# A graph convolution block on one core: linear layers, self rows and batch norm sums moved, tile by tile, into the edge aggregation

## The chip, the cores and the metric

The kernel runs on one core of one Trainium2 chip. The metric is the device time of one execution in microseconds (us). Below, "engine" means TensorE (PE, with its weight loads PEld), VectorE (DVE), ScalarE (ACT), GpSimd (POOL) or the queue of SyncE (SP).

## The reference

There are 6250 nodes with 256 features and 100,000 edges, sorted by destination, each with a weight. The block is a two-layer graph convolution with batch norm, and then a mixture of eight experts:

```python
def gcn_conv(x, src, dst, w, W, b, n):          # src, dst, w include one self edge of weight 1 per node
    xw = x @ W
    deg = segment_sum(w, dst)
    dinv = where(deg > 0, rsqrt(deg), 0.0)
    return segment_sum(xw[src] * (dinv[src] * w * dinv[dst])[:, None], dst) + b

h = layernorm(x)
out = gcn_conv(relu(gcn_conv(h, W1, b1)), W2, b2)
out = (out - out.mean(0)) * rsqrt(out.var(0) + 1e-5) * gamma + beta
x = x + relu(out + h)
x = x + top2_experts(layernorm(x))              # gate, 8 experts, exact gelu
```

## The kernel before, in words

**Tiles.** The nodes are padded to 49 tiles of 128 rows. X holds all tiles with a node per partition (49 x 256 columns), ACC holds the aggregate transposed (a feature per partition, two halves, 49 x 128 columns each). Because aggregation and linear layer commute, each layer first sums rows scaled by `dinv` and then multiplies by the weights.

**Edges.** The edges are cut into 784 tiles of 128, in 56 groups of 14 tiles (GT). A group's destinations span fewer than 128 nodes from a base `base_f[g]` that the data give. The first 16 groups (DG, "dense") go another way than the last 40 (GG, "gathered"):

- *Dense*: their weights are added up per pair (source, destination) and scattered by POOL, 224 indirect DMAs (L479), into a zeroed table in DRAM, which SP had filled (L358). SP reads it back in 196 units of 128x512 (L374, seven slots), and PE multiplies each unit with one tile of X (`dense`, L1272) into banks 6 and 7: 49 units make a block, 4 blocks a layer, and DVE adds a finished block to ACC (`add_block`, L923).
- *Gathered*: POOL fetches the source rows with 14 indirect DMAs per group (L492) into one of two buffers. DVE builds 14 one-hot matrices with the weights (`build`, L908), PE sums the group in 28 matmuls (L1287) into banks 0 to 3, and DVE adds the result to ACC at the group's base (`add_group`, L932). POOL may fill a buffer again once PE has signalled that the group in it is summed (`summed`).

**Order in a group.** The order is written out by hand. For group k DVE runs `build(k+1)`, then any finished block, then waits for `summed` and runs `add_group(k)`. PE runs tile j of the group, and after some of them a dense unit. Before the first group of layer 0 PE does 74 units by themselves (`BEFORE`); after that `PER_GROUP = (4, 5)` units go with each group, so layer 0 has dense units until group 30, and layer 1 until group 39.

**Around a layer.** Layer 0 begins with rows of X scaled by DVE and ACT, their store to a table in DRAM by SP (L381), and the self rows: PE transposes each tile of X (L1260, banks 4 and 5) and DVE copies it to ACC (L901). After its last group comes the linear layer, one tile after another: PE multiplies (L1308, banks 6 and 7), DVE scales and adds the bias into `tmp` (L971), ACT applies relu and scales into X (L623). Every seven tiles SP stores a chunk of X (L386). POOL's gathers of layer 1 wait for the last of these stores. The self rows of layer 1 follow on PE and DVE in the same way as before.

After the last group of layer 1 come the linear layer (L1308, DVE L982 back into ACC), with POOL adding up the rows (L512); PE reduces the sum (L1322), DVE forms the mean (L988) and subtracts it from ACC (L992), ACT squares (L632), PE adds up the squares (L1322), DVE forms the variance (L995), ACT takes the root (L635), DVE the reciprocal (L997) and the scale (L998, L1006). For the residual ACT rebuilds the normalized input (L644), POOL adds beta (L519), DVE adds the two (L1011). Router and experts follow, unchanged by the diff.

**The start.** Duplicate pairs within the dense edges are found by comparing each key with its 40 neighbours (MAXIN), eight at a time, in five passes on DVE: compare (L781), weights of equal ones (L783), a maximum over the eight (L784) and a sum over the eight (L787); L789 to L791 combine the passes. From this come the cells and weights that POOL scatters (L794 to L807). DVE and PE then sum the degrees group by group (L839 to L847, L1224), while POOL scatters.

Of the kernel before, what the change touches and what calls it, by code (L numbers as in the profile page):

```python
# [23 lines left out]
ASLOTS = 7  # L24
LN_EPS = 1e-05
# [25 lines left out]
def gnn_ffn(nc, x, src, dst, edge_weight, g_W1, g_b1, g_W2, g_b2, g_gamma, g_beta,  # L51
# [27 lines left out]
    UNITS = NB * NT  # L79
    GG = NG - DG  # L80
# [8 lines left out]
    with ExitStack() as ctx:  # L89
# [20 lines left out]
        parts = arena[:, at + 8 * RW:at + (8 + MAXIN // 8) * RW]  # L110
        assert (8 + MAXIN // 8) * RW <= 2 * GT * P
# [32 lines left out]
        eq8 = early(8 * (HALO + RW))  # L144
        had = early(MAXIN // 8 * RW)
# [59 lines left out]
        b1rows, sd_b = ln, mean_b  # L205
# [43 lines left out]
        sum_done, centred, sq_ready, sq_used = sem("sum_done"), sem("centred"), sem("sq_ready"), sem("sq_used")  # L249
# [18 lines left out]
        Q = NT  # L268
        BEFORE = (74, 0)
        PER_GROUP = (4, 5)  # L270

        def units_of(layer):
            

            n, plan = BEFORE[layer], []
            for g in range(GG):
                m = min(PER_GROUP[layer], UNITS - n) if g < GG - 1 else UNITS - n
                plan.append((n, m))
                n += m
            return plan  # L280
        SLOT_CH = [(NCH + 1) // 2, NCH // 2]
# [23 lines left out]

        def prior(q, j):


            return q + 1 if j == 0 else q
# [7 lines left out]
        with nc.Block() as block:  # L317
# [3 lines left out]
            def _(sp):  # L321
# [62 lines left out]
                for c in range(NCH):  # L384
                    sp.wait_ge(y_ready, 1 + CH * (c + 1))
# [51 lines left out]
            def _(pool):  # L437
# [66 lines left out]
                pool.wait_ge(agg_done, 2)  # L504
                g.memset(tmp[:, :], 0.0).then_inc(z_added, 1)
                with pool.Fori(0, NCH) as c:
                    for j in range(CH):
                        q = c * CH + j
                        pool.wait_ge(lin_used, q + (Q + 2))
                        pool.wait_ge(z_added, prior(q, j))  # L510
                        z = tmp[:, (j % 2) * D:(j % 2 + 1) * D].rearrange("p (c n) -> p c n", c=KC)
                        g.tensor_tensor(z, z, acc[:, :, bass.ds(q * P, P)], ALU.add).then_inc(z_added, 1)  # L512


# [57 lines left out]
            def _(act):  # L572
# [42 lines left out]
                act.sem_inc(y_ready, 1)  # L615
                for c in range(NCH):
                    for j in range(CH):
                        t = CH * c + j
                        if c + j == 0:
                            for n in range(2):  # L620
                                act.wait_ge(y_stored[n], 16 * SLOT_CH[n])
                        act.wait_ge(lin_used, 1 + t + 1)
                        a.activation(X[:, t * D:(t + 1) * D], tmp[:, (j % 2) * D:(j % 2 + 1) * D], ACT.Relu,  # L623
                                     scale=dinv[:, t:t + 1]).then_inc(y_ready, 1)


                with act.Fori(0, NCH) as c:
                    act.wait_ge(centred, c * 2 + 2)
                    for j in range(CH):
                        q = c * CH + j  # L630
                        act.wait_ge(sq_used, q + 1)
                        a.activation(slot(j).rearrange("p (c n) -> p c n", c=KC),  # L632
                                     acc[:, :, bass.ds(q * P, P)], ACT.Square).then_inc(sq_ready, 1)
                act.wait_ge(bn_var, 1)
                a.activation(sd_b[:, :], sd_b[:, :], ACT.Sqrt).then_inc(bn_sd, 1)  # L635
# [17 lines left out]

                norm_x(0)
                norm_x(1)
# [55 lines left out]
            def _(dve):  # L711
# [14 lines left out]
                dve.sem_inc(lin_used, 1)  # L726
# [24 lines left out]
                seen, first = eq8[0:DR, 0:RH], eq8[0:DR, RH:2 * RH]  # L751
# [429 lines left out]
            def _(pe):  # L1181
# [131 lines left out]
                for c in range(NCH):  # L1313
                    for j in range(CH):
                        linear(0, CH * c + j, j, W1g)
# [134 lines left out]
```

## Time and profile before

| | us |
|---|---|
| three executions, median (lowest, highest) | 3095.94 (3092.03, 3101.72) |
| the profiled execution | 3096.93 |
| its span, first to last instruction | 3095.1 |
| busy in it: PE, PEld | 2158.0, 1539.0 |
| busy in it: POOL, DVE, ACT | 1676.4, 901.8, 377.0 |
| mean granted clock of TensorE, share of full speed | 0.889 |

No engine is busy throughout, so the shares alone say little: the profile has to be read stage by stage. The rows quoted below are from the view of busy time by stretch and from timelines of single engines. In a timeline a row gives the start, the duration, the engine, the line, the operation with output and input, how often it is merged in the row, and in square brackets the idle time of the engine before it and what ended it. "Remote" means that the releaser is not among the recorded work, and "issue" that the engine waited for nothing that the profile shows. Starts are us from the beginning of the span.

### The profile page before, as it was taken

To read this page: it belongs to the slowest core of one execution; us is meant where nothing else is said; L and a number is where in the kernel's file an instruction comes from. 1 tells how busy PE (TensorE), PEld (TensorE's weight loads), DVE (VectorE), ACT (ScalarE), POOL (GpSimd) and SP (SyncE) were. 2 spreads that over 40 slices of the span, in tenths; PEclk is the share of its full clock that TensorE was granted. 3 is DMA by queue.
4 is the path that set the end of the run, shared out by engine and by line. 5 is a ranking of instruction groups with operands and counts; after the bars stand their busy time and mean duration, and the time that the engine had idled before them with its cause. 6 is when DMAs were issued, how large, how long until landed. Compare 5 with 4: busy or idle time off the path is not lost.

```text
span 3095.1 us, 34624 instructions
## 1 busy us (share of the span) xinstructions
PE 2158.0 (70%) x10692; PEld 1539.0 (50%) x10693; DVE 901.8 (29%) x2587; ACT 377.0 (12%) x1053; POOL 1676.4 (54%) x1782
## 2 busy tenths in 40 slices
PE   0100046998888788646598788888888666899897
PEld 0100033455555555535365455555555562788887
DVE  8700055011222211212332212222123676233332
ACT  6000001000000000001200000000000562333333
POOL 1677703016666666663346666666665430566665
PEclk9999999998888888767889899999999755999999
DMA  9940005544544444332445555555555023677775
GB/s 325 329 144 1 0 0 163 158 136 143 145 145 141 143 142 144 95 92 80 131 123 158 147 154 157 156 155 155 153 160 168 24 77 103 169 189 175 180 176 135
DMA packets 264392, 431.24 MB, mean 139 GB/s; under 512 B 39664, under 2 KB 147887, under 8 KB 264143
## 3 DMA queue, kind: packets, MB, share of 16 engines
q1 hardware_dynamic: 181455, 253.80, 26.1%
q0 software_dynamic: 81088, 173.80, 21.9%
q10 hardware_dynamic: 1728, 2.13, 0.2%
q8 instruction: 64, 1.05, 0.1%
q14 instruction: 57, 0.47, 0.0%
HBM read 339.36 MB, written 91.16 MB: 139 GB/s over the span
## 4 chain that ended last, share of the span: by engine, by line
another core or an unknown queue 28%; PE 23%; POOL 17%; DVE 13%; issue 11%; DMA 6%; POOLq 1%; DVEq 1%; SPq 1%; ACT 1%; ACTq 0%
POOL arena L492 14%; PE psum L1272 8%; PE psum L1287 4%; DMA ACC<-rows_for_experts,ACC 4%; DVE arena L908 3%; PE psum L1308 3%; PE psum L1394 2%; PE psum L1402 2%; POOL out_dram L558 2%; PE psum L1369 2%; DMA out_dram<-ACC 1%; PE psum L1224 1%; DVE ACC L845 1%; PE psum L1322 1%
## 5 line engine op out<-in xcount | busy, mean ns | idle before, releaser
L492 POOL DMA_INDIRECT arena<-conv_rows,edge_cols x1120 | 1059.4, 946 | 887.7 <-issue 318.7
L1287 PEld LDWEIGHTS psum<-arena 128*128 128x128 f32 x4480 | 640.9, 209 | 501.6 <-issue 484.8
L1287 PE MATMUL psum<-arena 128*128 128x128 f32 x4480 | 683.4, 296 | 289.9 <-issue 277.3
L1272 PE MATMUL psum<-arena,X 128*128 128x512 f32 x1568 | 815.5, 653 | 43.6 <-DVE ACC L923 26.4
L1272 PEld LDWEIGHTS psum<-arena,X 128*128 128x128 f32 x1568 | 303.3, 211 | 307.3 <-issue 273.3
L932 DVE TENSOR_TENSOR ACC<-ACC,psum 128x256 f32 x80 | 33.8, 422 | 1226.0 <-remote 1085.4
L479 POOL DMA_INDIRECT pair_weights<-scale_b,mean_b x224 | 229.5, 1025 | 156.3 <-DVE mean_b L807 88.3
L908 DVE TENSOR_SCALAR arena<-iota,edge_cols 128x128 f32<-128x128 f32 x1120 | 294.4, 370 | 0.3
L1224 PE MATMUL psum<-ACC 128*128 128x6 bf16 x784 | 56.1, 202 | 318.1 <-DVE ACC L845 299.0
L1394 PE MATMUL psum<-ACC,arena 128*128 128x128 f32 x1680 | 215.8, 284 | 0.2 <-DVE ACC L1154 0.2
L1224 PEld LDWEIGHTS psum<-ACC 128*128 128x128 bf16 x784 | 51.5, 159 | 322.8 <-DVE ACC L845 303.2
L558 POOL DMA_INDIRECT out_dram<-ACC x105 | 167.7, 1597 | 74.2 <-issue 49.2
L1394 PEld LDWEIGHTS psum<-ACC,arena 128*128 128x128 f32 x1680 | 206.8, 201 | 0.6 <-issue 0.6
L1402 PE MATMUL psum<-arena,ACC 128*128 x840 | 199.9, 381 | 0.2 <-ACT ACC L689 0.2
L1402 PEld LDWEIGHTS psum<-arena,ACC 128*128 128x128 f32 x840 | 152.7, 192 | 17.2 <-issue 0.6
L546 POOL DMA_INDIRECT ACC<-rows_for_experts,ACC x105 | 104.9, 999 | 84.8 <-DVE ACC L1141 51.0
L623 ACT ACTIVATE X<-tmp,dinv 128x256 f32<-128x256 f32 x49 | 24.9, 508 | 991.1 <-DVE tmp L971 991.1
L689 ACT ACTIVATE ACC<-psum,b1e 128x128 f32<-128x128 f32 x420 | 119.8, 369 | 164.5 <-PE psum L1394 130.8
L632 ACT ACTIVATE edge_cols<-ACC 128x256 f32 x49 | 18.8, 413 | 915.4 <-DVE ACC L992 914.8
L1172 DVE TENSOR_TENSOR ACC<-psum,b2e 128x256 f32<-128x256 f32 x105 | 44.7, 426 | 267.9 <-PE psum L1402 211.8
L842 DVE COPY ACC<-psum 128x6 f32 x56 | 9.1, 162 | 275.0 <-remote 263.2
L1260 PE MATMUL psum<-ident,X 128*128 128x128 f32 x196 | 50.3, 384 | 52.0 <-DVE ACC L901 27.3
(259 smaller groups left out, 1410.3 us busy)
## 6 DMA issues: line engine op xcount, KB each, us to landing
arena<-pair_weights SPq DMA_DIRECT2D x392, 256.0 KB
arena<-in_L_ffn_W_dram SPq DMA_DIRECT2D x113, 512.0 KB, 7.8
pair_weights<-zeros SPq DMA_DIRECT2D x4, 12544.0 KB, 60.5
arena<-conv_rows,edge_cols POOLq DMA_INDIRECT x1120
conv_rows<-X SPq DMA_DIRECT2D x14, 896.0 KB, 4.8
X<-in_x_dram SPq DMA_DIRECT2D x12, 896.0 KB, 10.4
rows_for_experts<-ACC SPq DMA_DIRECT2D x7, 910.0 KB, 4.3
out_dram<-X SPq DMA_DIRECT2D x6, 896.0 KB
```

What stands on the lines that cost most here:

```text
L479: pool.indirect_dma_start(pairs, bass.IndirectOffsetOnAxis(cell_i[:, t:t + 1], 0), cell_w[:, t:t + 1], None).then_inc(paired[b], 16)
L492: pool.indirect_dma_start(G[:, n * D:(n + 1) * D], None, y_tab[layer], bass.IndirectOffsetOnAxis(srcT[:, t:t + 1], 0)).then_inc(gathered[n ...
L546: pool.indirect_dma_start(xs[:, u * DX:(u + 1) * DX], None, rows_x, bass.IndirectOffsetOnAxis(slot_i[:, n:n + 1], 0)).then_inc(xs_in[u], 16)
L558: pool.indirect_dma_start(out, bass.IndirectOffsetOnAxis(slot_i[:, n:n + 1], 0), ys[:, u * D:(u + 1) * D], None, bounds_check=N - 1, oob_i ...
L689: ins = a.activation(hT[:, slot * H + c * P:slot * H + (c + 1) * P], psum[:, 2 + slot, c * P:(c + 1) * P], ACT.Gelu, bias=b1e[:, bass.ds(e ...
L908: v.tensor_scalar(S[:, n * P:(n + 1) * P], iota[:, 0:P], dst_rel[:, t:t + 1], wT[:, t:t + 1], ALU.is_equal, ALU.mult).then_inc(s_ready, 1)
L1224: ins = m.matmul(bank(2 + h, 6), hot[:, :, j], w_group[:, (h * GT + j) * 6:(h * GT + j + 1) * 6], start=(j == 0), stop=(j == GT - 1))
L1272: ins = m.matmul(bank(6 + c, BW), X[:, t * D + c * P:t * D + (c + 1) * P], A_in[:, u * BW:(u + 1) * BW], start=(t == 0), stop=(t == NT - 1))
L1287: ins = m.matmul(bank(2 * (k % 2) + c, P), G[:, n * D + c * P:n * D + (c + 1) * P], S[:, n * P:(n + 1) * P], start=(j == 0), stop=(j == GT ...
L1308: ins = m.matmul(bank(6 + j % 2, D), acc[:, k, bass.ds(q * P, P)], W[:, k * D:(k + 1) * D], start=(k == 0), stop=(k == KC - 1))
L1394: ins = m.matmul(psum[:, 2 + s, c * P:(c + 1) * P], w1s[:, s4 * KC * H + k * H + c * P:s4 * KC * H + k * H + (c + 1) * P], xsT[:, s * D + ...
L1402: ins = m.matmul(bank(4 + s, D), hT[:, s * H + c * P:s * H + (c + 1) * P], w2e[:, bass.ds(e * (HC * D) + c * D, D)], start=(c == 0), stop= ...
```

## The change

1. **Linear layers inside the aggregation.** Groups of edges are sorted by destination, so a tile of ACC is complete once the groups and dense blocks that reach it are added. `finish_of` works out, from a pace of 112 nodes a group (PACE) with a slack of 80, in which group each tile can be finished. In layer 0 that is from group 25 on (all four blocks must be in), three tiles a group, 45 in all; 4 remain for after the last group. In layer 1 it is from group 4 on, mostly one tile a group, three in groups 10, 20 and 30, 40 in all; 9 remain. PE does a tile's `linear` after edge tile j = 2, 6 or 10 of the group, in banks 4 and 5. DVE runs `finish` after `build(k+1)` and before `add_group(k)`. A new check sets the flag for the general path if a group's base is over 80 nodes off the pace.
2. **Next self rows.** With tile i of layer 0's linear layer PE also transposes the finished tile i-3 of X (banks 6 and 7), and DVE copies it to ACC. Only the last three are left for after.
3. **Dense units.** `PER_GROUP` becomes (5, 5), so that layer 0's dense work ends at group 24.
4. **Batch norm sums with a shift.** The mean of layer 1's first finished tile is subtracted from that tile, and from the bias of all later ones. DVE adds up the rows and the squares (which ACT makes) tile by tile. At the end two pairs of matmuls reduce both, and the variance is E[z^2] - E[z]^2. The subtraction of the mean, the pass of squares and POOL's sums are gone; the mean goes into beta instead, so that POOL's addition of beta now waits for the scale.
5. **Tree sums for duplicates.** The compare result becomes bf16, and the reductions over eight become three additions (maxima) of halves and one into a running result.

```diff
+SLACK = 80
+    PACE = GT * P * N // E
-        PER_GROUP = (4, 5)
+        PER_GROUP = (5, 5)
+        TURN_LAG = 3
 # duplicates (DVE), in each of the five passes
                     chain(v.tensor_tensor(same, key[:, 0:SPAN].unsqueeze(1).broadcast_to([DR, 8, SPAN]),
                                           sliding(key, d0, 8, 1, SPAN), ALU.is_equal))
                     v.tensor_tensor(wsame, same[:, :, HALO:SPAN], sliding(wrow, HALO + d0, 8, 1, RW), ALU.mult)
-                    chain(v.tensor_reduce(had[0:DR, c * RW:(c + 1) * RW],
-                                          sliding(eq8[0:DR, :], HALO - d0, 8, SPAN - 1, RW).rearrange("p d i -> p i d"),
-                                          AX_X, ALU.max))
-                    chain(v.tensor_reduce(parts[0:DR, c * RW:(c + 1) * RW], wsame.rearrange("p d i -> p i d"),
-                                          AX_X, ALU.add))
-                v.tensor_reduce(eq8[0:DR, 0:RW], had[0:DR, :].rearrange("p (c i) -> p i c", i=RW), AX_X, ALU.max)
-                chain(v.tensor_reduce(eqw[0:DR, 0:RW], parts[0:DR, :].rearrange("p (c i) -> p i c", i=RW), AX_X, ALU.add))
-                v.tensor_tensor(eqw[0:DR, RW:2 * RW], eqw[0:DR, 0:RW], wrow[:, HALO:SPAN], ALU.add).then_inc(pairs_summed, 1)
+                    chain(v.tensor_tensor(had3[:, 0:4], sliding(eq8[0:DR, :], HALO - d0, 4, SPAN - 1, RW),
+                                          sliding(eq8[0:DR, :], HALO - d0 + 4 * (SPAN - 1), 4, SPAN - 1, RW), ALU.max))
+                    v.tensor_tensor(had3[:, 4:6], had3[:, 0:2], had3[:, 2:4], ALU.max)
+                    chain(v.tensor_tensor(wsame[:, 0:4], wsame[:, 0:4], wsame[:, 4:8], ALU.add))
+                    v.tensor_tensor(had3[:, 6], had3[:, 4], had3[:, 5], ALU.max)
+                    chain(v.tensor_tensor(wsame[:, 0:2], wsame[:, 0:2], wsame[:, 2:4], ALU.add))
+                    v.tensor_tensor(had[0:DR, :], had3[:, 6], had3[:, 6] if c == 0 else had[0:DR, :], ALU.max)
+                    chain(v.tensor_tensor(wsame[:, 0], wsame[:, 0], wsame[:, 1], ALU.add))
+                    chain(v.tensor_tensor(wsum[0:DR, :], wsame[:, 0], wrow[:, HALO:SPAN] if c == 0 else wsum[0:DR, :],
+                                          ALU.add))
+                v.tensor_copy(had_f[0:DR, :], had[0:DR, :]).then_inc(pairs_summed, 1)
 # DVE, tile by tile
+                def finish(layer, i):
...
+                    dve.wait_ge(lin_done, n + 1)
+                    if layer == 0:
+                        if i >= 2:
+                            dve.wait_ge(y_ready, i - 1)
+                        v.scalar_tensor_tensor(out=tmp[:, (i % 2) * D:(i % 2 + 1) * D], in0=bank(4 + n % 2, D),
+                                               scalar=dinv[:, t:t + 1], in1=b1g[:, :],
+                                               op0=ALU.mult, op1=ALU.add).then_inc(lin_used, 1)
+                        if i >= TURN_LAG:
+                            take_self(1, i - TURN_LAG, FINISH[0][0][i - TURN_LAG], 6)
+                    else:
...
+                            dve.wait_ge(lin_used, n + 1)
+                            dve.wait_ge(z_added, i)
+                            z = z_sum.rearrange("p (c n) -> p c n", c=KC)
+                            v.tensor_tensor(z, z, out_rows, ALU.add).then_inc(z_added, 1)
+                            add_square(i - 1)
...
+                            for i in FINISH[layer][1][k]:
+                                finish(layer, i)
                             add_group(k)
                         dve.wait_ge(added, GG * (layer + 1))
+                        v.memset(dscr[:, :], 0.0).then_inc(agg_done, 1)
+                        finish_rest(layer, NT - len(FINISH[layer][2]), chain_fast)
 # PE, tile by tile
+                def linear(layer, i):
+                    t, n, W = FINISH[layer][0][i], NT * layer + i, (W1g, W2g)[layer]
+                    if n >= 2:
+                        pe.wait_ge(lin_used, n - 1)
...
+                    if layer == 0 and i >= TURN_LAG:
+                        turn_self(1, i - TURN_LAG, FINISH[0][0][i - TURN_LAG], 6)
...
+                                if j % 4 == 2 and j // 4 < len(FINISH[layer][1][k]):
+                                    i = FINISH[layer][1][k][j // 4]
+                                    blocks = NB if layer == 0 else blocks_under(FINISH[1][0][i])
+                                    if DG * layer + blocks:
+                                        pe.wait_ge(dense_added, DG * layer + BG * blocks)
+                                    linear(layer, i)
 # scale (DVE); POOL's additions of beta wait for bn_set
                 dve.wait_ge(sum_done, 2)
+                chain(v.tensor_scalar(mean_b[:, :], bank(6, D), 1.0 / N, None, ALU.mult))
+                chain(v.tensor_tensor(scale_b[:, :], mean_b[:, :], mean_b[:, :], ALU.mult))
+                chain(v.scalar_tensor_tensor(out=scale_b[:, :], in0=bank(7, D), scalar=1.0 / N, in1=scale_b[:, :],
+                                             op0=ALU.mult, op1=ALU.subtract))
+                chain(v.tensor_scalar(scale_b[:, :], scale_b[:, :], 0.0, BN_EPS, ALU.max, ALU.add))
+                v.tensor_copy(dscr[:, :], zeros[:, 0:1]).then_inc(bn_var, 1)
                 dve.wait_ge(bn_sd, 1)
-                chain(v.reciprocal(scale_b[:, :], sd_b[:, :]))
+                chain(v.reciprocal(scale_b[:, :], sd_b))
                 chain(v.tensor_tensor(scale_b[:, :], scale_b[:, :], gam[:, :], ALU.mult))
+                chain(v.tensor_tensor(mean_b[:, :], mean_b[:, :], scale_b[:, :], ALU.mult))
+                v.tensor_tensor(bet[:, :], bet[:, :], mean_b[:, :], ALU.subtract).then_inc(bn_set, 1)
```

## Rows read from the trace of the kernel before

**Rows 1.** Busy time by stretch: from, to, length; PE, PEld, DVE, ACT, POOL (count), clock, DMA.
```profile
674.00:1450.00 776.00, 579.98 (x2659) 410.77 (x2657) 158.06 (x584) 0.00 (x0) 503.25 (x532) 0.81 0.44 128
1571.00:2352.00 781.00, 652.36 (x2949) 428.57 (x2948) 157.50 (x582) 0.00 (x0) 502.44 (x532) 0.92 0.52 152
```
**Rows 2.** Timeline of DVE, two groups of layer 0 and two of layer 1.
```profile
875.73 0.42 DVE L932 TENSOR_TENSOR ACC<-ACC,psum 128x256 f32 x1 [16.18 <-remote]
895.96 0.42 DVE L932 TENSOR_TENSOR ACC<-ACC,psum 128x256 f32 x1 [16.22 <-remote]
...
1610.83 0.42 DVE L932 TENSOR_TENSOR ACC<-ACC,psum 128x256 f32 x1 [16.20 <-remote]
...
1631.07 0.42 DVE L932 TENSOR_TENSOR ACC<-ACC,psum 128x256 f32 x1 [16.23 <-remote]
```
**Rows 3.** Timeline of POOL at the end of one group's gathers in layer 1.
```profile
1627.21 0.95 POOL L492 DMA_INDIRECT arena<-conv_rows,edge_cols  x1 [0.30 <-issue]
1631.21 0.95 POOL L492 DMA_INDIRECT arena<-conv_rows,edge_cols  x1 [3.05 <-remote]
```
**Rows 4.** Timeline of DVE, the last groups of layer 0, eight group intervals apart.
```profile
1299.62 0.42 DVE L932 TENSOR_TENSOR ACC<-ACC,psum 128x256 f32 x1 [12.57 <-remote]
...
1449.76 0.42 DVE L932 TENSOR_TENSOR ACC<-ACC,psum 128x256 f32 x1 [9.39 <-PE psum L1287]
```
**Rows 5.** Timelines of DVE, ACT and POOL between the layers.
```profile
1452.18 0.48 DVE L971 SCALAR_TENSOR_TENSOR tmp<-psum,dinv,b1g 128x256 f32<-128x256 f32 x1 [1.33 <-PE psum L1308]
...
1501.48 0.51 ACT L623 ACTIVATE X<-tmp,dinv 128x256 f32<-128x256 f32 x1 [0.43 <-DVE tmp L971]
...
1507.76 0.94 POOL L492 DMA_INDIRECT arena<-conv_rows,edge_cols  x1 [65.67 <-DMA conv_rows<-X]
...
1570.52 0.94 POOL L492 DMA_INDIRECT arena<-conv_rows,edge_cols  x1 [28.03 <-PE psum L1287]
```
**Rows 6.** Timeline of DVE, self rows of layer 1 before and during POOL's gathers.
```profile
1504.41 0.76 DVE L901 COPY ACC<-psum 128x256 f32<-128x256 f32 x2 [0.26 <-PE psum L1260]
...
1542.94 0.42 DVE L901 COPY ACC<-psum 128x256 f32<-128x256 f32 x1 [4.48 <-remote]
```
**Rows 7.** Timelines of DVE and POOL after the last group of layer 1.
```profile
2357.69 0.06 DVE L961 MEMSET dscr<- 128x1 f32 x1 [0.60 <-DVE ACC L932]
2359.80 0.48 DVE L982 SCALAR_TENSOR_TENSOR ACC<-psum,dinv,b2g 128x256 f32 x1 [2.05 <-PE psum L1308]
...
2440.05 1.75 DVE L997 RECIPROCAL scale_b<-mean_b 128x256 f32<-128x256 f32 x1 [0.48 <-ACT mean_b L635]
2440.58 10.44 POOL L519 TENSOR_TENSOR edge_cols<-edge_cols,bet 128x256 f32<-128x256 f32 x10 [28.43 <-ACT edge_cols L644]
2447.39 3.06 DVE L1011 TENSOR_TENSOR edge_cols<-edge_cols,ACC 128x896 f32<-128x896 f32 x2 [2.05 <-POOL edge_cols L519]
```
**Rows 8.** Timeline of DVE at the start: one pass for duplicates, the end, a bf16 product.
```profile
28.16 2.68 DVE L781 TENSOR_TENSOR ACC<-arena 112x2432 f32<-112x2432 f32 x1
...
33.09 3.62 DVE L784 TENSOR_REDUCE ACC<-ACC 112x256 f32<-112x2048 f32 x1
36.74 3.65 DVE L787 TENSOR_REDUCE arena<-arena 112x256 f32<-112x2048 f32 x1
40.42 2.69 DVE L781 TENSOR_TENSOR ACC<-arena 112x2432 f32<-112x2432 f32 x1
...
89.36 2.31 DVE L789 TENSOR_REDUCE ACC<-ACC 112x256 f32<-112x1280 f32 x1
...
94.27 0.39 DVE L796 SCALAR_TENSOR_TENSOR arena<-psum,edge_cols 128x224 f32<-128x224 f32 x1
...
260.16 1.09 DVE L845 TENSOR_TENSOR ACC<-ACC 128x1792 bf16<-128x1792 bf16 x1
```
**Rows 9.** Timeline of POOL: a scatter beside L829 and one beside no DVE work.
```profile
105.22 2.82 POOL L479 DMA_INDIRECT pair_weights<-scale_b,mean_b  x1 [0.30 <-issue]
...
182.24 0.96 POOL L479 DMA_INDIRECT pair_weights<-scale_b,mean_b  x1 [0.30 <-issue]
```

More of the change, by code:

```diff
@@ L280, in units_of, with finished, blocks_under, finish_of @@
             return plan
+        def finished(g):
+            return NT if g == NG else max(0, min(NT, (PACE * g - SLACK) // P))
+        def blocks_under(t):
+            g = next(g for g in range(NG + 1) if finished(g) > t)
+            under = [d for d in range(min(g, DG)) if PACE * d + SLACK + P > P * t]
+            return under[-1] // BG + 1 if under else 0
+        def finish_of(layer):
+            plan = units_of(layer)
+            ends = [next((k for k, (n, m) in enumerate(plan) if n + m >= (b + 1) * NT), GG - 1) for b in range(NB)]
+            ends = [-1 if (b + 1) * NT <= BEFORE[layer] else e for b, e in enumerate(ends)]
+            free = []
+            for t in range(NT):
+                g = next(g for g in range(NG + 1) if finished(g) > t)
+                blocks = NB if layer == 0 else blocks_under(t)
+                free.append(max(g - DG + 1, ends[blocks - 1] + 1 if blocks else 0, 0))
+            order = sorted(range(NT), key=lambda t: (0 if layer == 0 else min(free[t], GG), t))
+            groups, n = [], 0
+            for k in range(GG):
+                most = 1 if layer == 1 and n == 0 else 2 if k in ends else 3
+                if layer == 1 and n == 1 and groups[-1]:
+                    most = 0
+                mine = []
+                while n < NT and len(mine) < most and free[order[n]] <= k:
+                    mine.append(n)
+                    n += 1
+                groups.append(mine)
+            return order, groups, list(range(n, NT))
+        FINISH = [finish_of(layer) for layer in range(2)]
         SLOT_CH = [(NCH + 1) // 2, NCH // 2]
@@ L501, in _ @@
                                 bass.IndirectOffsetOnAxis(gstg[:, 0:1], 0)).then_inc(gen_gathered, 16)
[L504 to L512, printed above, removed]
+                pool.wait_ge(bn_set, 1)
                 for c in range(NCH):
@@ L1207, in _ @@
                 pe.wait_ge(pairs_summed, 1)
-                for x, rows in enumerate((eq8[0:DR, 0:RW], eqw[0:DR, RW:2 * RW])):
+                for x, rows in enumerate((had_f[0:DR, :], wsum[0:DR, :])):
                     for h in range(2):
@@ new lines, in mean_of_first, with linear_rest @@
+                def mean_of_first():
+                    t = FINISH[1][0][0]
+                    pe.wait_ge(lin_used, NT + 1)
+                    m.matmul(bank(4 + (NT + 1) % 2, D).rearrange("p (c n) -> p c n", c=KC), ones[:, :],
+                             acc[:, :, t * P:(t + 1) * P], start=True, stop=True).then_inc(first_mean, 1)
+                def linear_rest(layer, first):
+                    for i in range(first, NT):
+                        if layer == 1 and i == 1:
+                            mean_of_first()
+                        linear(layer, i)
+                    if layer == 0:
+                        for i in range(NT - TURN_LAG, NT):
+                            turn_self(1, i, FINISH[0][0][i], 6)
```

227 lines of the change are left out of this document (126 added, 101 removed).

## Prediction

> **What bounds the kernel now.** The view of busy time by stretch comes first. In both aggregations [rows 1] no engine is full: over 781 us of layer 1 PE is busy 652, POOL 502, DVE 158, ACT 0. So what counts is what a group waits for, and the rest of the time lies in stretches where one engine works alone. DVE's timeline shows how long a group is: two `add_group` of layer 0, with four dense units between them, stand 20.23 us apart, two of layer 1, with five, 20.24 [rows 2]. A fifth unit costs nothing, so PE's work isn't the limit. POOL's timeline shows what is [rows 3]: a gather occupies 0.95 us and 0.30 us of issue, 14 of them 17.5 us, and before the first gather of the next group POOL stands 3.05 us, 2.75 more than between two others; 17.5 + 2.75 = 20.25. It waits for the signal that PE has summed the group before. That DVE's wait ends by "remote" says that PE's signal came later than its recorded work. Where dense units are gone, at the end of layer 0, eight intervals take 150.14 us, 18.8 each [rows 4].
>
> Between the layers POOL stands still. From layer 0's last addition (1449.76) to the first gather of layer 1 (1507.76) are 58.0 us: 49 tiles of linear layer at 1.0 us each, then 6.3 us from the last relu over the store to the gather [rows 4, 5]. The third set of gathers starts 62.8 us after the first [rows 5]: PE first turned 49 self rows, with a handshake of 0.5 us a tile before the gathers run and 4.5 us during them [rows 6], and only then summed group 0. After layer 1's last group 82.4 us pass until the reciprocal [rows 7]. At the start 12.26 us go to each of five passes over duplicates, and 4.9 us to the end of them [rows 8]; POOL's scatter waits for that, and the rest of the program for the scatter or for DVE's degree loop, which starts behind the same work.
>
> **The change, part by part.** The sum is made against the profiled execution, 3096.93 us; the median of the three is 1.0 lower.
>
> *Duplicates.* Each pass loses two reductions, 3.62 + 3.65 = 7.27 us. It gains two operations of 1024 columns, two of 512 and four of 256. At the rate between L796 (224 columns, 0.39) and L781 (2432, 2.68), 0.16 us + 1.04 ns a column, that is 2 x 1.22 + 2 x 0.69 + 4 x 0.42 = 5.5 us: 1.8 saved, 9 in five passes. If the four bf16 maxima run at L845's rate (1792 columns in 1.09), they cost 1.5 us instead of 2.75, and 6 more are saved. The end goes from 4.9 to a copy of 0.3. The new check on group bases adds five operations of one to 56 columns, about 1.1 us. Together -12 to -19; I take **-15**, as nothing else waits there. Scatter and degree loop both move with it.
>
> *Layer 0's groups.* Five units instead of four cost nothing by [rows 2]. Groups 25 to 39 lose their dense units, but each gets three linear layers, three transposes and the handshakes PE to DVE to ACT. They are no longer than a group with five units (20.2), if the 18 us of a group hold three handshakes; no shorter than 18.8. Before, nine groups ran at 18.8. At 20.2 for all, the eight intervals cost 8 x 1.4 = **+11**; at 18.8 for all, six further groups gain 6 x 1.4 = 8. I take +11, since PE's late signals, not its load, made the 20.2. The other bound is a later gather: the handshake of 4.5 us [rows 6] three times is 13.5, which still fits in 20.2 beside DVE's 14 one-hots (3.7 us), but not with much to spare; +34 if each of the 15 groups grows by half of one such handshake.
>
> *Between the layers.* 58.0 becomes four tiles at 1.2 us with their self rows, 1.4 to the first and one to the last relu, and 6.3 for store and gather: 13.8, so **-44**. SP's earlier stores go out during the groups; its loads of dense units for layer 1 stand behind the last store in its queue as before. Bounds -48 (last chunk's store alone) and -35 (the 6.3 doubled by seven tiles to store).
>
> *First groups of layer 1.* Only three self rows come after. Group 0 is summed while group 1 is gathered, so the third set starts two periods after the first: 2 x 20.2 = 40 instead of 62.8, **-23** (-25 to -10: in the first period PE also begins dense units).
>
> *Layer 1's groups.* 40 tiles of linear layer go in: a few matmuls each on PE, which a fifth unit shows to be no limit. DVE: `finish` 0.48, z 0.42, square 0.42, beside 16 us of idle a group; its wait for `linear` lies between `build(k+1)` and `add_group(k)`, so what queues behind it is `add_group`, whose bank PE does not want for the next group. ACT had nothing. What may cost is POOL. A scatter that ran beside DVE's L829 (two inputs in SBUF) took 2.82 us, one beside none 0.96 [rows 9], a stretch of up to 0.67 of L829's 2.77. Adding rows (z, squares) are such operations, 80 in all of 0.42 us; `add_group`, with one input in PSUM, is not. 80 x 0.15 = **+12**; 0 if POOL's 3.05 us of waiting takes it up, +22 at 0.67 x 0.42 each, +50 if each holds POOL for a gather's half.
>
> The Trainium skill speaks against this part ("SBUF — State Buffer", "Who interferes with whom"): a VectorE instruction with two inputs in SBUF contends with a GpSimd instruction that reads SBUF, and a holder of the shared ports blocks the other for its whole length. By it each of the 80 would hold POOL for up to 0.42 us, 34 us, and the sum would be 22 higher; [rows 9] agree with a stretch, and at 1.9 of 2.8 us not with the whole length.
>
> *After layer 1.* 82.4 us become 2.1 to the first result [rows 7], nine tiles at 0.48 + 0.42 + 0.42 + some 0.13 between = 13.0, last square 0.9, two pairs of matmuls 1.7, four small operations on the mean and variance 1.9, root 0.5: 20.3, so **-62**. Against it, POOL's addition of beta ran while DVE made the scale; the first seven tiles (1.04 us each) now begin only when the shifted beta is there. L1011 came 7.3 us after the reciprocal's start; now 1.75 + 0.4 + 0.9 + 7.3 = 10.4 or a little more, **+4**. Bounds for both: -64 to -48 (nine tiles at 2.6 if ACT's squares are waited for singly).
>
> Sum: -15 + 11 - 44 - 23 + 12 - 58 = **-117**: 3096.9 - 117 = 2980 for the profiled execution, 2979 for the median.
>
> **The rivals.** (1) *The groups grow.* Late signals of PE and shared ports make each of layer 1's 40 groups, or layer 0's last 15, longer by 0.5 to 1.5 us: +30 to +65 over the forecast, 3010 to 3045. For it: the pause of 3.05 shows that the signal is on the path, and each `linear` adds waits in PE's queue ahead of it. Against: the fifth unit cost nothing. (2) *The groups without dense units keep their pace* of 18.8, and adds cost nothing: 11 + 8 + 12 less, about 2948. For it: [rows 4]; against: late signals. (3) *Slower.* The three handshakes in each of layer 0's groups 25 to 39 are in series on PE: `linear(i)` waits for DVE to empty the bank two tiles back, DVE for PE's late signal and for ACT. If such a signal arrives only when POOL's issue pauses, a group needs an extra turn of gathers, 20.2 us; 15 x 20.2 = 303 on the sum gives 3283. It decides from 117 / 15 = 7.8 us a group. For it: 4.5 us a handshake, and PE's signals that come only in POOL's pauses; against: [rows 6] already ran under gathers, so the delay is a few us, not a whole period. (4) *The change doesn't take hold*: a base over 80 off the pace sends all to the general path; bases of 112 a group by evenly spread destinations make that remote, and it would be many times slower.
>
> **How the numbers follow.** Forecast 0.68 (its own range 2955 to 3008, from the bounds of the terms, few of which will lie at the same end), rival 1 0.18, rival 2 0.07, rival 3 with smaller kin 0.06, rival 4 0.01. A difference of 0.3%, 9 us, is what a measurement of this kernel can tell. All but rivals 3 and 4 are beyond it on the fast side: faster 0.93, same 0.01, slower 0.06. The range 2945 to 3035 takes in rival 2 and most of rival 1, and leaves out the rest.
>
> **What would show it.** L796 at some 79 us instead of 94.27. `add_group` 20.2 apart throughout, also in groups 25 to 39. From layer 0's last addition to the next gather 14 us, third set of gathers 40 us later. L492 near 0.95 us on average in layer 1; well over 1.0 would mean the ports. From the memset after layer 1 to the reciprocal 20 us. Group intervals above 21 us, or waits of DVE for `lin_done` that end after the last gather of a group, would say that rival 1 or 3 holds; a gap of 30 us or more between the layers would make my view of the stores wrong.

## The result, and the profile after

The changed kernel took 2994.11 us (median of four, 2982.97 to 2998.0) against 3098.29 for the kernel before on the same chip: a ratio of 0.9663, interval 0.9638 to 0.9687. The profiled execution took 2998.0 us (span 2996.2), 99 less than that of before.

The timelines of DVE and POOL at the start of the changed kernel answer to [rows 8]: one pass for duplicates with its tree sums, the first scatter, and the last step of the degree loop.

```profile
26.87 2.68 DVE L818 TENSOR_TENSOR ACC<-arena 112x2432 bf16<-112x2432 f32 x1
...
31.80 0.69 DVE L821 TENSOR_TENSOR ACC<-ACC 112x1024 bf16<-112x1024 bf16 x1
...
32.86 1.22 DVE L824 TENSOR_TENSOR arena<-arena 112x1024 f32<-112x1024 f32 x1
...
36.17 2.69 DVE L818 TENSOR_TENSOR ACC<-arena 112x2432 bf16<-112x2432 f32 x1
...
76.58 1.28 POOL L520 DMA_INDIRECT pair_weights<-scale_b,mean_b  x1 [67.58 <-DVE mean_b L846]
...
399.46 0.16 DVE L881 COPY ACC<-psum 128x6 f32 x1 [9.23 <-remote]
...
455.29 0.16 DVE L881 COPY ACC<-psum 128x6 f32 x1
...
487.18 0.99 POOL L533 DMA_INDIRECT arena<-conv_rows,edge_cols  x1 [115.27 <-DMA conv_rows<-X]
```

A pass is 9.30 us instead of 12.26; maxima in bf16 take little over half of the f32 additions of the same size (0.69 against 1.22). POOL's first scatter starts at 76.6 instead of 97.3. But the first gather, at 487.2, is only 12.2 us earlier than before (499.4).

The view of busy time by stretch, for both aggregations, answers to [rows 1], with the same columns.

```profile
664.00:1447.00 783.00, 611.43 (x2914) 438.42 (x2913) 192.48 (x669) 22.64 (x45) 504.04 (x532) 0.85 0.46 134
1500.00:2327.00 827.00, 699.18 (x3111) 460.77 (x3109) 209.61 (x710) 16.68 (x40) 504.90 (x532) 0.90 0.49 145
```

The timelines of DVE, POOL and ACT answer to [rows 2] to [rows 5]: two groups early in layer 1, two later ones, and what lies between the layers.

```profile
1447.86 0.42 DVE L1032 TENSOR_TENSOR ACC<-ACC,psum 128x256 f32 x1 [0.84 <-PE psum L1406]
...
1453.28 0.51 ACT L651 ACTIVATE X<-tmp,dinv 128x256 f32<-128x256 f32 x1 [0.57 <-DVE tmp L950]
...
1460.21 1.05 POOL L533 DMA_INDIRECT arena<-conv_rows,edge_cols  x1 [24.19 <-DMA conv_rows<-X]
...
1540.53 0.42 DVE L1032 TENSOR_TENSOR ACC<-ACC,psum 128x256 f32 x1 [16.33 <-remote]
...
1560.76 0.42 DVE L1032 TENSOR_TENSOR ACC<-ACC,psum 128x256 f32 x1 [16.21 <-remote]
...
1830.39 0.42 DVE L1032 TENSOR_TENSOR ACC<-ACC,psum 128x256 f32 x1 [13.50 <-PE psum L1406]
...
1854.78 0.42 DVE L1032 TENSOR_TENSOR ACC<-ACC,psum 128x256 f32 x1 [15.66 <-PE psum L1406]
1854.92 0.95 POOL L533 DMA_INDIRECT arena<-conv_rows,edge_cols  x1 [7.21 <-PE psum L1406]
```

The gap between the layers is gone: 12.4 us from the last addition to the first gather instead of 58.0. Early groups of layer 1 stand 20.23 us apart, as before. From about 1830 on they don't: 24.39 here. And the wait is named otherwise: POOL waits 7.21 us, and what ends it is no longer "remote", a late signal, but PE's matmul itself. In the stretch of layer 1 above, 21 of POOL's waits end that way, 107.0 us in all, and 17 by "remote"; in the kernel before it was 3 and 35. From 1830.5 to the last set of gathers at 2294.2 the sets start 20.3 to 28.1 us apart, 22.1 on average.

DVE's timeline after the last group answers to [rows 7].

```profile
2327.90 0.06 DVE L1053 MEMSET dscr<- 128x1 f32 x1
2330.01 0.48 DVE L957 SCALAR_TENSOR_TENSOR ACC<-psum,dinv,mean_b 128x256 f32<-128x256 f32 x1 [2.04 <-PE psum L1355]
...
2340.97 0.95 DVE L975 TENSOR_TENSOR tmp<-tmp,ln 128x256 f32<-128x256 f32 x2
...
2348.74 0.42 DVE L1075 TENSOR_SCALAR mean_b<-psum 128x256 f32<-128x256 f32 x1 [6.82 <-PE psum L1443]
...
2351.08 1.75 DVE L1082 RECIPROCAL scale_b<-ln 128x256 f32<-128x256 f32 x1 [0.48 <-ACT ln L684]
...
2360.82 3.05 DVE L1098 TENSOR_TENSOR edge_cols<-edge_cols,ACC 128x896 f32<-128x896 f32 x2 [4.08 <-POOL edge_cols L550]
```

By stage, from the two traces, against the terms of the forecast:

| stretch | before | after | change | forecast |
|---|---|---|---|---|
| start to the first gather | 499.4 | 487.2 | -12.2 | -15 |
| to layer 0's last addition | 950.3 | 960.7 | +10.4 | +11 |
| to the first gather of layer 1 | 58.0 | 12.4 | -45.6 | -44 |
| to the third set of gathers | 62.8 | 39.9 | -22.9 | -23 |
| to layer 1's last addition | 786.2 | 827.4 | +41.2 | +12 |
| to the reciprocal | 83.4 | 23.7 | -59.7 | -62 |
| to the end | 655.1 | 645.1 | -10.0 | +4 |

One term is far off: layer 1's groups.

### The profile page after: what moved, and what is told of

It reads as the page before. It is cut to its first block, busy times and chain, and to the rows that moved or that the text cites. A ratio compares the mean times of both kernels' runs of the same rounds, so it can differ in the third digit from the quotient of the medians.

```text
span 2996.2 us, 34126 instructions
## 1 busy us (share of the span) xinstructions
PE 2110.1 (70%) x10594; PEld 1505.7 (50%) x10595; DVE 903.2 (30%) x2713; ACT 378.4 (13%) x1053; POOL 1639.9 (55%) x1732
## 4 chain that ended last, share of the span: by engine, by line
PE 43%; another core or an unknown queue 23%; DVE 13%; issue 11%; DMA 6%; POOL 3%; POOLq 1%; DVEq 1%; ACT 1%; SPq 0%; ACTq 0%
PE psum L1391 17%; PE psum L1406 13%; DMA ACC<-rows_for_experts,ACC 4%; PE psum L1355 3%; DVE arena L1008 3%; PE psum L1510 2%; PE psum L1518 2%; POOL out_dram L589 2%; PE psum L1485 2%; PE psum L1344 1%; DMA out_dram<-ACC 1%; DVE ACC L884 1%; PE psum L1310 1%; PE psum L1501 1%
## 5 line engine op out<-in xcount | busy, mean ns | idle before, releaser
L1406 PEld LDWEIGHTS psum<-arena 128*128 128x128 f32 x4480 | 629.0, 207 | 390.1 <-issue 380.1
L1406 PE MATMUL psum<-arena 128*128 128x128 f32 x4480 | 663.5, 293 | 202.8 <-issue 189.5
L1510 PE MATMUL psum<-ACC,arena 128*128 128x128 f32 x1680 | 208.3, 277 | 0.2 <-DVE ACC L1241 0.2
L1510 PEld LDWEIGHTS psum<-ACC,arena 128*128 128x128 f32 x1680 | 198.9, 194 | 0.6 <-issue 0.6
L661 ACT ACTIVATE ln<-ACC 128x256 f32<-128x256 f32 x49 | 20.4, 417 | 866.8 <-issue 520.1
L1355 PE MATMUL psum<-W1g,ACC 128*128 128x256 f32 x196 | 71.4, 474 | 31.8 <-issue 17.3
## 6 DMA issues: line engine op xcount, KB each, us to landing
X<-in_x_dram SPq DMA_DIRECT2D x12, 896.0 KB, 10.4
```

The lines of the kernel that those rows point to most:

```text
L1355: ins = m.matmul(bank(4 + n % 2, D), acc[:, k, t * P:(t + 1) * P], W[:, k * D:(k + 1) * D], start=(k == 0), stop=(k == KC - 1))
L1406: ins = m.matmul(bank(2 * (k % 2) + c, P), G[:, n * D + c * P:n * D + (c + 1) * P], S[:, n * P:(n + 1) * P], start=(j == 0), stop=(j == GT ...
L1510: ins = m.matmul(psum[:, 2 + s, c * P:(c + 1) * P], w1s[:, s4 * KC * H + k * H + c * P:s4 * KC * H + k * H + (c + 1) * P], xsT[:, s * D + ...
```

## The experiments

Theory A: PE is too full in layer 1. Rival B: DVE's new additions, with two inputs in SBUF, hold POOL. Rival C: the groups are longer for another reason that has nothing to do with the linear layers. The runs fell on four chips, none of them that of the first measurement: e1 to e4 on one, b2, e5 and e6 on the second, e7, b3 and e8 on the third, e9 on the last. Ratios are to the kernel before on the same chip. Where e1 to e4 and e9 are compared with the changed kernel, that stands on another chip, b2_after's or b3_after's.

**e1_lin1_last**

```diff
                 groups.append(mine)
+            if layer == 1:
+                return order, [[] for _ in range(GG)], list(range(NT))
```

> The changed kernel with all 49 linear layers of layer 1 after the last group, with the shifted sums as they are; layer 0 as changed. Theory A (PE is too full: a linear layer added to a group with five dense units and the pause of some 3 us near the end of each group's gathers pushes PE past the 20.2 us that the gathers take): the groups of layer 1 go back to 20.2 to 20.3 us, third set of gathers to last addition 786 us instead of 827, the 40 tiles moved behind the last group cost 40 x 1.2 = 48 us there. In all +7 (+2 to +12) against the changed kernel. Rival B (the adds of DVE with two inputs in SBUF slow POOL): the same numbers, so this run alone does not part the two. Rival C (the groups of layer 1 are longer for another reason, e.g. the earlier start against the stream of dense units): groups stay at 827, and the run is +48.

**e2_no_adds**

```diff
-                            v.tensor_tensor(z, z, out_rows, ALU.add).then_inc(z_added, 1)
+                            v.tensor_tensor(z_sum[:, 0:1], z_sum[:, 0:1], out_rows[:, 0, 0:1], ALU.add).then_inc(z_added, 1)
-                        v.tensor_tensor(sq_sum, sq_sum, sq, ALU.add).then_inc(sq_used, 1)
+                        v.tensor_tensor(sq_sum[:, 0:1], sq_sum[:, 0:1], sq[:, 0:1], ALU.add).then_inc(sq_used, 1)
```

> The changed kernel, with DVE's additions of rows and of squares cut to one column each (the sums for the batch norm are left out but for that column). Theory A (PE too full): the groups stay long, 820 to 830 us from the third set of gathers to the last addition, and only some 6 us go after the last group, where DVE's three operations a tile set the pace: -4 to -10 in all. Rival B (DVE's adds hold POOL or DVE): back to 786 to 792, -40 to -50 in all.

**e3_spread16**

```diff
-        BEFORE = (74, 0)
+        BEFORE = (74, 16)
-                m = min(PER_GROUP[layer], UNITS - n) if g < GG - 1 else UNITS - n
+                m = min(PER_GROUP[layer] - (layer == 1 and g % 2 == 1), UNITS - n) if g < GG - 1 else UNITS - n
```

> The changed kernel with 16 dense units of layer 1 ahead of its first group, and then five and four units in turn instead of five. Theory A: PE has idle time between the last self row and the first gathered tile (12 us), which takes some six units; the other ten push group 0 by at most 19 us, of which part is cover; with 4.5 units a group on average PE fits in 20.2, so the groups take 790 to 800 instead of 827 and the whole is -15 to -35. Rival B or C: the groups stay near 827, and the whole is 0 to +15.

**e4_dup_old**: the tree sums back to the two reductions a pass and the two at the end, in f32, as in the diff read backwards.

> The changed kernel with the reductions of before for the duplicates. The first scatter comes 20 us later (97). If the degree loop's own queue of halves left over at the scatter's end is the reason that only 12 of the 21 us were kept, the first gather comes 12 (8 to 21) us later and the run is +12. If the loss of 8 us had another cause, it is +20.

The first thing measured was not asked for: on this chip the kernel before took 2610.78 us, not 3098. Signals were prompt: but for one wait of 8.3 us in e3 POOL never waited for PE, and a group took its 14 gathers, 17.5 us. So A could show only if PE were too full even for that, and what is expected above for late signals could not be tested. All further runs met chips of this kind.

| run | ratio (interval) | third gathers to last addition | last addition to reciprocal |
|---|---|---|---|
| e1_lin1_last | 0.9686 (0.9657 to 0.9716) | 680.9 | 72.7 |
| e2_no_adds | 0.9505 (0.947 to 0.9539) | 681.0 | 23.0 |
| e3_spread16 | 0.954 (0.9509 to 0.957) | 681.1 | 23.2 |
| e4_dup_old | 0.9585 (0.9555 to 0.9615) | 683.2 | 23.6 |

For comparison both kernels were traced on the next chip, together with the same undoing for layer 0 and a milder form of e3.

> The kernel before once more, for a trace on this chip. In the four runs above PE's signals were not late and a group took 17.5 us, the time of its 14 gathers, instead of 20.2; the kernel before took 2611 us beside them, not 3098. Expected on such a chip: groups of 17.5 us in both layers, degree loop over long before the scatter ends, 58 us between the layers, 83 us from the last addition to the reciprocal. On a chip as in the prediction: the rows of the prediction.

> The changed kernel once more. On a chip with groups of 17.5 us: the duplicates are then off the path only if the degree loop were, so their 20 us are kept whole; between the layers -44, first groups of layer 1 -20, layer 1's groups 681 us from the third set of gathers to the last addition with or without linear layers in them (0), end -60: some -125 against the kernel before on this chip, ratio 0.952, and about 20 us under the run with the old duplicates. On a chip as in the prediction: ratio 0.966.

**e5_lin0_last**: as e1_lin1_last, with `layer == 0`.

> The changed kernel with all 49 linear layers of layer 0, and the self rows that go with them, after the last group; layer 1 as changed. The gap between last addition and first gather goes from 12 back to 58 us or more, since the transposes now go beside (45 tiles at 1.0 to 1.2 us: +45 to +54). Groups 25 to 39 of layer 0: on a chip with groups of 17.5 us they stay at 17.4 (0); on a chip as in the prediction they go from 19.2 to 18.8 on average (-6). In all +40 to +54.

**e6_spread6**: as e3_spread16, with `BEFORE = (74, 6)` and `g % 4 == 3`.

> The changed kernel with six dense units of layer 1 ahead of its first group, and then four units in every fourth group, five in the others. On a chip as in the prediction, theory A (PE too full): the six units cost nothing, as PE stands idle for 12 us there, and the groups take 800 to 815 us instead of 827: -12 to -27. On a chip with groups of 17.5 us POOL's gathers are the bound, not PE: 0 (-4 to +4).

| run | time, us | ratio (interval) | last addition to first gather | third gathers to last addition |
|---|---|---|---|---|
| b2_before | 2610.84 | | 59.5 | 678.7 |
| b2_after | 2482.10 | 0.9513 (0.948 to 0.9545) | 12.3 | 682.0 |
| e5_lin0_last | 2532.21 | 0.9717 (0.9687 to 0.9747) | 63.2 | 681.6 |
| e6_spread6 | 2476.81 | 0.9497 (0.9467 to 0.9526) | 12.4 | 679.4 |

What follows. On such chips the change gives 4.9% and not 3.4. Its traces put -18.8 us on the start, -47.2 on the gap between the layers, nothing on the first gathers of layer 1 (35.3 before, 35.1 after, where I had expected -20: the self rows had not held them up), +3.3 on layer 1's groups and -62.9 up to the reciprocal. Taking the linear layers of layer 1 out of the groups costs 48.7 us behind them and gives back 1 (e1); those of layer 0 cost 50.9 (e5); the old reductions start the first gather at 392.3 instead of 372.1 and cost 0.7% (e4). So the start and both linear layers are worth close to what was forecast for them. Whether an unfinished degree loop ate 8 of the 20 us at the start of the first chip, which e4 was to tell, it can't tell here: the gathers follow the scatter at once. Sixteen units ahead of layer 1 are too many: the third set of gathers came 43.1 us after the first instead of 35.1 (e3).

Rival B has fallen on both kinds of chip. The view of costliest groups gives the mean of one gather (line, engine, operation, busy us, mean ns, idle before them and what ended it), here for the changed kernel in the first measurement and then on the second chip.

```profile
L533 POOL DMA_INDIRECT arena<-conv_rows,edge_cols x1120 | 1062.6, 949 | 876.8 <-issue 318.2 <-PE psum L1406 261.0 <-remote 158.2
```

```profile
L533 POOL DMA_INDIRECT arena<-conv_rows,edge_cols x1120 | 1066.1, 952 | 357.4 <-issue 340.9 <-DMA conv_rows<-X 16.5
```

In layer 1 alone, in the first measurement, a gather took 949 ns in the changed kernel and 945 before it: 560 x 4 ns = 2 us, not 12 or more. The additions do hold POOL, but briefly and seldom: the 52 gathers beside one took 976 ns on average and 1197 at most. And on the prompt chip e2, without the additions, left the groups at 681.0, as e1 and e3 did. The Trainium skill ("SBUF — State Buffer", "Who interferes with whom"), by which each addition could have held POOL for its 0.42 us, gave too much here: 80 of them cost some 2 us. The idle time shows the other matter: 261 us of POOL waiting for PE's own work (141 of them before the third set of layer 0, where the kernel before has 139) and 158 for late signals on the first chip, while neither is listed on the second.

For A there remained the question how full PE is. Two kernels load it on purpose.

**e7_double_linear**

```diff
-                    for k in range(KC):
+                    for k in range(KC if layer == 0 else 2 * KC):
+                        k = k % KC
```

> The changed kernel with every linear layer of layer 1 computed twice over into the same bank (1.0 us more on PE for each tile, the result the same). Theory A (PE too full), on a chip with groups of 17.5 us: PE's own work in a group is then 9.4 (five dense units) + 7 (14 tiles) + 2 = 18.4 us at full clock, over the 17.5 of the gathers, so the groups take 700 to 730 us from the third set of gathers to the last addition instead of 682, and nine tiles after it 3 us more: +20 to +50. On a chip as in the prediction: +30 to +60 over the changed kernel. If PE had room in a group, as the prediction took it, +3 on either.

**e9_four_linear**: the same with `4 * KC`.

> The changed kernel with every linear layer of layer 1 computed four times over into the same bank (2.6 us more on PE a tile, the result the same); the double one had left the groups at 17.5 us. By the steps of the timeline a group is 14/3 x 1.34 + 4.9 x 1.72 = 14.7 us of PE, 15.5 with one linear layer, 16.4 with two, 18.1 with four. Theory A's reading (PE limits the groups once its own time with its pauses passes that of the gathers) on a chip with groups of 17.5 us: 0.6 us on each of 40 groups and a backlog at blocks' ends, third set of gathers to last addition 700 to 715 instead of 682, and 2.6 us on nine tiles after it, 23: +40 to +60 in all. On a chip as in the prediction, where the pauses take 3 us of a group and the lower clock some 2: +90 to +120 in the groups. If PE were not what a group can come to wait for: +23 in all.

e7: 0.9556 (0.9532 to 0.958), the groups 683.5 us, hardly longer than without it, and 27.8 from the last addition to the reciprocal. My expectation of +20 to +50 missed. These two stretches are 4.5 us longer than in b3_after, close to the +3 expected if PE has room; the medians differ by 11 us with intervals that overlap. I had given PE too much time for a group. e9: 0.9734 (0.9713 to 0.9754), the groups 719.6, then 40.0, 37.6 and 16 us more than in b2_after. Here POOL waited for PE 20 times, 41.4 us in all: the load has become the bound. In all e9 is 59 us over b2_after, within the expected +40 to +60, though its groups passed the expected 700 to 715. DVE's timeline of e9 in layer 1 shows PE's own pace with four linear layers, and that of the kernel before on the second chip its pace with none, while it still had units to catch up on:

```profile
1514.57 0.42 DVE L1032 TENSOR_TENSOR ACC<-ACC,psum 128x256 f32 x1 [5.37 <-PE psum L1407]
...
1532.86 0.42 DVE L1032 TENSOR_TENSOR ACC<-ACC,psum 128x256 f32 x1 [8.88 <-PE psum L1407]
...
1551.15 0.42 DVE L1032 TENSOR_TENSOR ACC<-ACC,psum 128x256 f32 x1 [8.88 <-PE psum L1407]
```

```profile
1204.88 0.42 DVE L932 TENSOR_TENSOR ACC<-ACC,psum 128x256 f32 x1 [10.73 <-PE psum L1287]
...
1219.72 0.42 DVE L932 TENSOR_TENSOR ACC<-ACC,psum 128x256 f32 x1 [10.81 <-PE psum L1287]
...
1234.56 0.42 DVE L932 TENSOR_TENSOR ACC<-ACC,psum 128x256 f32 x1 [10.73 <-PE psum L1287]
```

18.29 us with four, 14.84 with none, so 0.86 for each linear layer, and 15.7 us for the changed kernel's group on PE at full clock (granted 1.00 in the stretches of these rows).

The busy time of layer 1's stretch on the second chip, the changed kernel and then the kernel before, with the columns of [rows 1]:

```profile
1127.00:1809.00 682.00, 625.89 (x3064) 420.74 (x3062) 207.75 (x696) 16.69 (x40) 506.58 (x532) 0.99 0.60 175
```

```profile
1193.00:1872.00 679.00, 604.79 (x2936) 396.79 (x2934) 158.09 (x578) 0.00 (x0) 505.23 (x532) 0.98 0.60 176
```

Nearly the same work took PE 626 us there and 699 on the first chip, 73 us or 1.8 a group more, at a granted clock of 0.99 against 0.90; for the kernel before it was 48 us (652.4 against 604.8), 1.2 a group. On the first chip PE also stands idle, 128 us in the stretch of layer 1 (827 - 699; in the kernel before 781 - 652 = 129). Much of this lies near the end of each set of gathers, where its matmuls come one by one. This timeline of PE in the kernel before shows it, beside a set whose gathers ran from 1897.55 to 1914.73:

```profile
1910.33 1.05 PE L1287 MATMUL psum<-arena 128*128 128x128 f32 x8
1911.22 1.88 PE L1272 MATMUL psum<-arena,X 128*128 128x512 f32 x4
1912.94 0.38 PE L1287 MATMUL psum<-arena 128*128 128x128 f32 x2
1913.78 0.27 PE L1287 MATMUL psum<-arena 128*128 128x128 f32 x1 [0.46 <-issue]
1914.52 0.35 PE L1287 MATMUL psum<-arena 128*128 128x128 f32 x1 [0.47 <-issue]
1915.88 0.27 PE L1287 MATMUL psum<-arena 128*128 128x128 f32 x1 [1.02 <-issue]
1917.28 1.23 PE L1287 MATMUL psum<-arena 128*128 128x128 f32 x7 [1.13 <-issue]
```

The row of 1910.33 ends the group; the matmuls that come one by one are already the next group's first. In the changed kernel (gathers from 1809.30 to 1826.50) the group's last two tiles fall into this pause, and PE starts again at half the pace (3.62 us for the four matmuls of a unit, which otherwise take 1.88):

```profile
1824.83 0.27 PE L1406 MATMUL psum<-arena 128*128 128x128 f32 x1
1826.24 0.48 PE L1406 MATMUL psum<-arena 128*128 128x128 f32 x2 [1.14 <-issue]
1828.33 0.37 PE L1406 MATMUL psum<-arena 128*128 128x128 f32 x1 [1.61 <-issue]
1829.04 1.22 PE L1406 MATMUL psum<-arena 128*128 128x128 f32 x4 [0.34 <-issue]
1830.05 3.62 PE L1391 MATMUL psum<-arena,X 128*128 128x512 f32 x4
1833.46 1.76 PE L1406 MATMUL psum<-arena 128*128 128x128 f32 x12
1835.05 1.88 PE L1391 MATMUL psum<-arena,X 128*128 128x512 f32 x4
```

These terms must not be added up and held against the 20.2 us: busy and idle time together fill any stretch, and 15.7 + 1.8 + 3.2 is only 827 / 40 again. What tells the room is how long before its signal arrives, that is, before `add_group`, a group's last matmul has ended:

| groups on the first chip | last matmul to `add_group`, us |
|---|---|
| before, layer 0, 8 to 29 (four units) | 8.2 (median) |
| before, layer 1, 3 to 8 (five units) | 6.3 (median) |
| after, layer 0, 15 to 23 (five units) | 6.1 (median) |
| after, layer 1, up to 15, one linear layer, away from a block's end (eight groups) | 4.1 to 5.7 |
| after, layer 1, 16 to 36 | 0.1 to 0.6 in 19 of 21 |

Each load brings the end closer to the signal, the fifth unit (1.72 us) too. In the rows of the kernel before the pause begins at 1913.3, 4.3 us before `add_group` at 1917.61, so by my estimate some 2 of the 6.3 us were room, and with a linear layer at most 1.4 were left. Once these are used up, the last matmuls of a group come to lie in the pause, POOL starts its next 14 gathers later, and what a block's addition adds in waiting (PE stood idle for 8.41 us at 1898, behind DVE) is not made good. That is theory A. Against rival C speak the groups without a linear layer: five units alone kept to 20.2 or 20.3 us in layer 0 but behind the ends of two blocks, and behind late group 36 group 37, which has none, was 5.2 us ahead of its signal again. All this is argued from that chip's trace and from PE's times on the others; no kernel could be run against it on a chip with late signals, so it isn't shown, and rival C isn't excluded there. Why signals are late on one chip and not on others, and what holds PE's matmuls up in the pauses, stays open as well.

Last, the milder spreading once more beside the changed kernel.

> The changed kernel once more, beside the next run. 0.951 of the kernel before on a chip with groups of 17.5 us, 0.966 on one as in the prediction.

> Six dense units of layer 1 ahead of its first group once more, for a closer comparison with the changed kernel on the same chip. On a chip with groups of 17.5 us: 3 to 8 us under the changed kernel, from the third set of gathers to the last addition 679 instead of 682. On a chip as in the prediction, by theory A 12 to 27 under it.

Changed kernel 2486.35 us, 0.9516 (0.9491 to 0.954); with six units ahead 2483.64, 0.9496 (0.9477 to 0.9516), groups of layer 1 680.5 against 682.7. Both times it was the faster one, by 5 and by 3 us, but the intervals overlap: no difference is shown. On a chip with late signals, where it would matter by theory A, it wasn't run.

## Why the prediction was right, and where not

The time, -99 us in the profiled execution against -117, and 2994 in a range of 2945 to 3035, was right; its terms were so in part, and luck had a share: half of the 29 us by which layer 1's groups missed was made up by the last stretch, 14 us under its term.

- *Between the layers* and *first groups of layer 1*: -45.6 and -22.9 for -44 and -23, by the steps given. The second exists only where handshakes during the gathers are slow; on the other chips it is nothing.
- *After layer 1*: -59.7 for -62. Two errors nearly cancel: a tile took 1.2 us instead of 1.45, and the matmuls for the two sums came after a wait of 6.8 us instead of 1.7. POOL's addition of beta cost 2.4 (9.7 from reciprocal to L1098 instead of 7.3) for 4.
- *Duplicates*: -20.7 at the first scatter, beyond the range of -12 to -19. The passes gave 14.7, as the maxima did run at bf16's rate, their end 4.7, and they began 1.3 earlier instead of 1.1 later. "Scatter and degree loop both move with it" failed on the first chip. While POOL scatters, DVE waits up to 37.9 us for a signal of PE, whose matmuls were then done for some 37; the steps left over are run off behind it, from 399.5 to 455.3 in the changed kernel (56 us), from 421.0 to 467.6 before (47). An earlier scatter met a loop that had got less far, and 12.2 were kept. On the other chips, where the gathers follow the scatter at once, 18.8 were.
- *Layer 0's groups*: +10.4 for +11, by luck. The eight intervals that the prediction read as 18.8 us each [rows 4] took 150.35 us in the changed kernel, for 150.14. Seven of them were 20.0 on average before it too, and only the last, behind which POOL gathers nothing, was short (9.8). Groups 25 to 39 took 288.4 us from the addition of group 24 to that of 39, before 291.4, so the three linear layers in each cost nothing; rival 3, the handshakes, didn't come. The rest lies in the groups before them, with a fifth unit: 496.2 us against 484.8. There POOL twice waited 5.9 and 7.2 us instead of 3.0, behind blocks' ends.
- *Layer 1's groups* is the step that failed, as rival 1 had it: "a fifth unit costs nothing, so PE's work isn't the limit", and then "a few matmuls each on PE, which a fifth unit shows to be no limit". That a load costs nothing shows that there is room for that load, not for the next. And the fifth unit did cost: [rows 2] are single intervals, and in layer 1 of the kernel before POOL also waited 6.07 us at 1775.90 and 4.91 at 1960.17, both ended by PE's matmul. PE's work was near the limit: by the estimate above some 2 us of room were left in a group, of which a linear layer takes 0.86, and what is lost at a block's end has to be made good from the rest. The term was given +12 for shared ports, which cost 2; it measured +41. Rival 1 gave shared ports a part in it, too.
- The last stretch, from the reciprocal on, is 10 us shorter, though the change leaves it alone but for the 2.4 above. In the traces of all other runs, with the change and without it, this stretch lies between 642.0 and 659.1 us, so the -10 are no more than it varies by. Without it the profiled execution would be at -89.

## What to carry to other kernels

Before moving work into the shade of another engine, look in every period of the trace, not in one, how long before the others need it that engine ends its part, and compare this with what you add; a load that cost nothing before is only a lower bound of the room. Busy and idle time added up tell nothing, as they always fill the period. When a wait's releaser in the profile turns from "remote" or a DMA into the engine's own instruction, that engine ends last, but need not be full: in the kernel before POOL waited 7.48 us for PE's matmul at 1341.97, when PE had been busy for 12.7 of 37.0 us and had no dense units, its matmuls coming one by one while POOL gathered two sets without a pause.

```profile
1341.97 0.94 POOL L492 DMA_INDIRECT arena<-conv_rows,edge_cols  x1 [7.48 <-PE psum L1287]
```

And an effect that rests on late signals should be expected to differ from one chip to another.

## What the runs showed of the hardware

The kernel before took 3098 us on one chip and 2610 to 2615 on four others. The difference lies where POOL issues indirect DMAs: 108.5 us up to the first gather (499.4 against 390.9), 243.2 from there to layer 0's last addition (950.3 against 707.1), 27.5 in the first two groups of layer 1 (62.8 against 35.3) and 107.5 in the others (786.2 against 678.7); the stretch from the reciprocal on differs by 4 (655.1 against 650.6). One gather took nearly the same (946 and 950 ns). Two things differed on PE. On the four chips `add_group` began 0.13 us after a group's last matmul had ended (in b2_before in 38 of the 40 groups of layer 1), on the first some 6 us after it. And on the first PE's matmuls came one by one, 0.7 to 2.8 us apart, from 14 to 16 us after the start of a set of gathers until POOL had stood still for 2.5 to 3.3 us; when POOL gathered two sets without a pause, this lasted from 1313.9 to 1337.8, 24 us.
